# A depthwise convolution of 32 taps in front of a transformer block: as one 32x32 triangular product per channel on TensorE, in place of shifted multiply-adds

## The chip, the cores and the metric

The kernel runs on one core of a Trainium2 chip. The metric is the device time of one execution in microseconds (us). A kernel's time is the median of its runs.

## The reference

x is 32 sequences (B) of 32 tokens (T) with 256 channels (C). `cond` (32 x 256) serves twice: as the 32 taps of a causal depthwise convolution over the tokens, and as the conditioning vector of a block with attention and an MLP, one row per sequence. All is float32.

```
x  = x + conv(x, cond)               # y[b,t,c] = sum_j cond[31-j,c] * x[b,t-j,c]
ada = cond @ ada_w + ada_b           # shift, scale, gate, twice
x1 = ln(x) * (1 + scale1) + shift1
q, k, v = split(x1 @ qkv_w + qkv_b)  # 16 heads of 128
a  = softmax(q k^T / sqrt(128)) v    # within each sequence of 32
h  = x + gate1 * (a @ out_w + out_b)
x2 = ln(h) * (1 + scale2) + shift2
h  = h + gate2 * (gelu(x2 @ ffn_w1 + ffn_b1) @ ffn_w2 + ffn_b2)
x  = x + h
```

## The kernel before, in words

Activations are held with channels in the 128 partitions (two tiles, `ct`) and the 1024 tokens along the free axis. The queues of the five engines are written out by hand, each in its own block (SyncE issues the loads, then GpSimd, ScalarE, VectorE, TensorE), and tied by semaphores; each engine goes through its list in order. A large product is made of three fp32r matmuls (`three`, L927, and `v_tile`, L934) from operands split into a high and a low part: ScalarE makes the high parts (`high_parts` of the weights, L333; `x1_high`, L376), GpSimd the low parts of the weights (L278), VectorE those of the activations (`x1_low`, L595).

The 16 heads come in four groups (`hg`) of four, the tokens in two halves (`u`) of 512, so there are eight units (hg, u). A unit projects twelve banks of q, k and v, makes the scores (L992, 32x32 blocks), and in between does the attention product (`attend`, L1006) and the output projection (`out_proj`) of the unit before it. Then come the second norm, the MLP and the stores.

At the start, x is loaded with tokens in partitions, in three chunks (`CHUNKS`: 256, 256 and 512 tokens), turned by TensorE in transposes (L839, L909) and copied to `x0`. The convolution is a sum over 31 lags and the token itself. Some lags go to TensorE (`PE_LAGS`: 12, 16 and 8 by chunk) as products with a diagonal matrix (`diag`, made by ScalarE, L342, and GpSimd, L270), accumulated in a bank (L853); the others go to VectorE as multiply-adds (L537) into `xc`. `conv_sum` (L547) adds the bank. Chunk by chunk the first norm follows: `mean` on TensorE (L863), `centre` (L553) on VectorE, `squares` (L371) on ScalarE, `var` (L874, L879) on TensorE, `var_eps` (L568) on VectorE, the power -1/2 (`rstd`, L284) on GpSimd, `spread` (L891) on TensorE, `norm`, `shift` (L582, L589) on VectorE. `modulation` (L899, added up in L602) gives shift, scale and gate from `cond`. The first half of the projections of unit (0,0) is done in two pieces, `project_chunk(0)` and `project_chunk(1)`; the convolution, norm and the rest of chunk 2 lie between these and the first attention products.

The order on TensorE ahead of unit (0,1), in the program's words:

```
conv(0), transposes of chunk 2, modulation(0), mean(0), conv(1) with var(0), spread(0)
project_chunk(0) with mean(1), var(1), spread(1); conv(2, 0, 4)
project_chunk(1) with scores(0, 0); conv(2, 4, ..); modulation(1)
mean(2), attend and out_proj of (0,0) with var(2), modulation(2), spread(2)
project(0, 1, ..) nine banks; scores(0, 1); three banks
```

## Time and profile before

| | us |
|---|---|
| median of 3 runs | 338.48 |
| lowest and highest run | 337.24, 339.4 |
| profiled execution, span from first to last instruction | 337.2 |
| TensorE matmul busy | 319.7 (95%) |
| TensorE weight load busy | 269.0 (80%) |
| VectorE, ScalarE, GpSimd busy | 180.0, 152.7, 80.8 |

The profile has one line for a group of instructions: source line, engine, operation, output <- input, partitions x elements, count, then the busy time. PE is TensorE, PEld its weight load, DVE VectorE, ACT ScalarE, POOL GpSimd, SP SyncE. An ordinary fp32 matmul of the program stands in the trace as two records, a transpose or an fp32r matmul as one. PEclk is the granted TensorE clock, 1.00 at 2.4 GHz and 0.50 at 1.2 GHz. "Idle before" names what ended an engine's idle time. Matmuls overlap, so a record's own time is longer than the step from one to the next; such steps are taken from the starts.

### The profile page before, as it was taken

To read this page: it belongs to the slowest core of one execution; us is meant where nothing else is said; L and a number is where in the kernel's file an instruction comes from. 1 tells how busy PE (TensorE), PEld (TensorE's weight loads), DVE (VectorE), ACT (ScalarE), POOL (GpSimd) and SP (SyncE) were. 2 spreads that over 40 slices of the span, in tenths; PEclk is the share of its full clock that TensorE was granted. 3 is DMA by queue.
4 is the path that set the end of the run, shared out by engine and by line. 5 is a ranking of instruction groups with operands and counts; after the bars stand their busy time and mean duration, and the time that the engine had idled before them with its cause. 6 is when DMAs were issued, how large, how long until landed. Compare 5 with 4: busy or idle time off the path is not lost.

```text
span 337.2 us, 6425 instructions
## 1 busy us (share of the span) xinstructions
PE 319.7 (95%) x2655; PEld 269.0 (80%) x2655; DVE 180.0 (53%) x354; ACT 152.7 (45%) x269; POOL 80.8 (24%) x78
## 2 busy tenths in 40 slices
PE   5969599999999999999999999999999999899994
PEld 4959496868888888888888888888898778588884
DVE  4959979866606224333441532631625699783232
ACT  6421032423366525526625535653443557742910
POOL 5606510031034103006303003500201444430400
PEclk9959789999999999999999999999999999999998
DMA  7822100010004202002300101210200000000011
GB/s 247 318 68 62 62 3 0 2 65 0 0 2 126 64 0 64 0 2 68 122 0 0 62 0 41 86 63 0 64 2 0 3 2 0 0 2 0 0 64 62
DMA packets 9607, 14.56 MB, mean 43 GB/s; under 512 B 520, under 2 KB 5744, under 8 KB 9584
## 3 DMA queue, kind: packets, MB, share of 16 engines
q1 hardware_dynamic: 9536, 14.19, 12.9%
q8 instruction: 17, 0.28, 0.3%
q14 instruction: 6, 0.05, 0.1%
q10 hardware_dynamic: 48, 0.03, 0.0%
HBM read 13.18 MB, written 1.05 MB: 42 GB/s over the span
## 4 chain that ended last, share of the span: by engine, by line
PE 79%; DVE 17%; issue 1%; DMA 1%; ACT 1%; DVEq 0%
PE bank L930 16%; PE bank L931 16%; PE bank L932 16%; PE bank L1006 7%; DVE xc L537 6%; PE bank L939 4%; PE bank L941 4%; PE bank L940 4%; PE bank L863 3%; PE bank L992 3%; PE bank L853 3%; DVE pt L642 2%; DVE yacc L747 1%; DVE xc L547 1%; DMA crow<-in_cond_dram 1%
## 5 line engine op out<-in xcount | busy, mean ns | idle before, releaser
L278 POOL TENSOR_TENSOR wl<-raw,wh 128x512 fp32r<-128x512 f32 x40 | 53.1, 1349 | 181.2 <-ACT wh L333 181.2
L930 PE MATMUL bank<-x1h,wl 128*128 128x512 f32 (+1 forms) x176 | 67.8, 385 | 0.0
L931 PE MATMUL bank<-x1l,wh 128*128 128x512 f32 (+1 forms) x176 | 65.9, 374 | 0.0
L932 PE MATMUL bank<-x1h,wh 128*128 128x512 f32 (+1 forms) x176 | 65.8, 374 | 0.0
L394 ACT ACTIVATE pool<-bank,bg 128x512 f32<-128x512 f32 x56 | 38.6, 688 | 57.3 <-PE bank L932 57.0
L653 DVE SCALAR_TENSOR_TENSOR ol<-bank,bT,oh 128x512 fp32r<-128x512 f32 x32 | 23.9, 749 | 46.8 <-ACT oh L423 46.0
L537 DVE SCALAR_TENSOR_TENSOR xc<-x,condT,xc 128x240 f32<-128x240 f32 (+32 forms) x114 | 39.4, 417 | 0.0
L930 PEld LDWEIGHTS bank<-x1h,wl 128*128 128x128 f32 x176 | 34.0, 193 | 6.3 <-issue 0.7
L931 PEld LDWEIGHTS bank<-x1l,wh 128*128 128x128 f32 x176 | 34.0, 193 | 5.8 <-issue 0.2
L932 PEld LDWEIGHTS bank<-x1h,wh 128*128 128x128 f32 x176 | 33.9, 193 | 5.7
L1006 PEld LDWEIGHTS bank<-pt,pool 128*128 128x128 f32 x256 | 31.9, 191 | 3.4 <-issue 0.9
L1006 PE MATMUL bank<-pt,pool 128*128 128x128 f32 x256 | 32.8, 276 | 0.6 <-DVE ol L653 0.4
L423 ACT ACTIVATE oh<-bank,bg 128x512 fp32r<-128x512 f32 x32 | 21.9, 687 | 22.3 <-PE bank L1006 22.3
L617 DVE TENSOR_REDUCE mx<-bank 128x16 f32<-128x512 f32 x8 | 5.5, 691 | 47.2 <-PE bank L992 47.2
L853 PE MATMUL bank<-x,diag 128*128 128x256 f32 (+23 forms) x144 | 30.5, 369 | 0.0
L853 PEld LDWEIGHTS bank<-x,diag 128*128 128x128 f32 x144 | 24.8, 202 | 4.8 <-issue 1.0
L930 PE MATMUL bank<-oh,wl 128*128 128x512 f32 x64 | 26.4, 412 | 0.0
L939 PE MATMUL bank<-wh,x1l 128*128 128x512 f32 x64 | 26.3, 411 | 0.0
L941 PE MATMUL bank<-wh,x1h 128*128 128x512 f32 x64 | 25.0, 391 | 0.0
L932 PE MATMUL bank<-oh,wh 128*128 128x512 f32 x64 | 25.0, 391 | 0.0
L931 PE MATMUL bank<-ol,wh 128*128 128x512 f32 x64 | 25.0, 390 | 0.0
L940 PE MATMUL bank<-wl,x1h 128*128 128x512 f32 x64 | 25.0, 390 | 0.0
(105 smaller groups left out, 450.8 us busy)
## 6 DMA issues: line engine op xcount, KB each, us to landing
raw<-in_L_cond_qkv_w_dram SPq DMA_DIRECT2D x12, 512.0 KB, 3.8
raw<-in_L_cond_out_w_dram SPq DMA_DIRECT2D x4, 512.0 KB, 3.4
raw<-in_L_cond_ffn_w_dram SPq DMA_DIRECT2D x4, 512.0 KB, 3.4
adaw<-in_L_cond_ada_w_dram SPq DMA_DIRECT2D x1, 1024.0 KB, 11.3
out_dram<-pool SPq DMA_DIRECT2D x4, 256.0 KB, 2.2
pool<-in_x_dram SPq DMA_DIRECT2D x2, 256.0 KB, 3.1
adaw<-in_L_cond_ada_w_dram SPq DMA_DIRECT2D x1, 512.0 KB, 5.3
pool<-in_x_dram SPq DMA_DIRECT2D x1, 512.0 KB, 6.1
```

What stands on the lines that cost most here:

```text
L278: g.tensor_tensor(wl[:, cols], raw[:, cols], wh[:, cols].bitcast(F32), ALU.subtract)\
L394: a.activation(dst, src, ACT.Identity, bias=bg[:, j // GH, j % GH:j % GH + 1])\
L537: v.scalar_tensor_tensor(out=acc[:, :, j:], in0=xs[:, :, :T - j], scalar=w, in1=acc[:, :, j:], op0=ALU.mult, op1=ALU.add).then_inc(s_cdve, 1)
L653: v.scalar_tensor_tensor(out=ol[:, h, :], in0=OB[h % 2][:, :], scalar=bT[:, bass.ds(group * GH + (2 * NH + h), 1)], in1=oh[:, h, :].bitcas ...
L853: m = pe.matmul(dst[:, :, j:], diag[:, CT * d + ct, :], xs[:, :, :T - j], start=(i == 0), stop=(i == last))
L930: pe.matmul(dst, wl[:, w_cols], a_hi, start=start, stop=False)
L931: pe.matmul(dst, wh[:, w_cols], a_lo, start=False, stop=False)
L932: return pe.matmul(dst, wh[:, w_cols], a_hi, start=False, stop=stop)
L939: pe.matmul(dst, x1l[:, kt, tk], wh[:, wc], start=(kt == 0), stop=False)
L940: pe.matmul(dst, x1h[:, kt, tk], wl[:, wc], start=False, stop=False)
L941: m = pe.matmul(dst, x1h[:, kt, tk], wh[:, wc], start=False, stop=(kt == CT - 1))
L1006: m = pe.matmul(OB[h % 2][:, t * P:(t + 1) * P], v_sb[:, hn, t, h * P:(h + 1) * P], pt[:, hn, h, t, :], start=True, stop=True)
```

## The change

The convolution becomes one product per channel c: the stationary operand is the 32x32 matrix `toep[s, u, c] = cond_pad[s + u, c]` (s the input token, u = 31 - t the output token counted from the end), zero where s + u > 31; the moving operand is that channel of x in all 32 sequences, with tokens in the partitions. `cond_pad` is `cond` with 31 rows of zeros behind it, written to DRAM by two DMAs of ScalarE's queue, and `toep` is loaded from it by one DMA whose rows overlap. x is loaded once, with the 32 tokens in 32 partitions (`xs`). TensorE first puts x itself, turned, into four banks (`XB`, L821), makes the 256 products (L836) into four other banks (`CB`), four channels in four column groups, and when ScalarE and VectorE have copied these to `conv_out`, it adds them to `XB` (`turn`, L849) by products with a 0/1 matrix `pick` that restores channel and token order. ScalarE and VectorE copy two of the sums each to `xc`. The diagonals, the multiply-adds, the copies to `x0` and `conv_sum` are gone. The norms of the three chunks are then done without a convolution between them, modulations 1 and 2 are one, and unit (0,1) has the order of the later units. The loads of the biases move from SyncE's to ScalarE's queue; `toep` stands ahead of the load of `ada_w`.

```diff
-            load_x(0)
-            load_x(1)
+            sp.dma_start(xs, x.rearrange("b t c -> t b c")).then_inc(s_x, 16)
+            sp.wait_ge(s_pad, 32)
+            sp.dma_start(toep[:, :, :].rearrange("p u c -> p (u c)"),
+                         bass.AP(cond_pad, 0, [[C, T], [1, T * C]])).then_inc(s_toep, 16)
             load_adaw(0, 0, ADA1 * P)
-            load_x(2)
...
             a.dma_start(crow[:, :], cond).then_inc(s_row[0], 16)
+            a.dma_start(cond_pad[0:T, :], cond).then_inc(s_pad, 16)
+            a.wait_ge(s_zr, 1)
+            a.dma_start(cond_pad[T:2 * T - 1, :], zrows[:, :]).then_inc(s_pad, 16)
...
+            def conv_copy(k):
+
+                a.wait_ge(s_cv, k + 1)
+                a.activation(conv_out[:, CBLK * k:CBLK * (k + 1), :],
+                             CB[k][:, :].rearrange("p (s b) -> p s b", b=B), ACT.Copy).then_inc(s_co[0], 1)
+
+            def xc_copy(n):
+
+                a.wait_ge(s_sel, n + 1)
+                a.activation(xc[:, :, XCH * n:XCH * (n + 1)],
+                             XB[n][:, :].rearrange("p (k t) -> p k t", k=CT), ACT.Copy).then_inc(s_xc[0], 1)
...
-            high_parts(0, range(0, 2))
+            conv_copy(0)
+            conv_copy(2)
+            xc_copy(0)
+            xc_copy(2)
             squares(0)
-            high_parts(0, range(2, 4))
+            high_parts(0, range(0, 4))
             group_biases(0, 0, 3)
-            high_parts(0, range(4, 5))
+            squares(1)
             x1_high(0)
-            high_parts(0, range(5, 6))
+            high_parts(0, range(4, 6))
...
+            pe.wait_ge(s_x, 16)
+            for n in range(NX):
+                for i in range(CT * XB_B):
+                    ct, b = divmod(i, XB_B)
+                    pe.matmul(XB[n][:, T * i:T * (i + 1)], xs[:, XB_B * n + b, P * ct:P * (ct + 1)], ident[0:T, 0:T],
+                              start=(i == 0), stop=False, skip_group_check=True)
...
+                for s in range(CBLK):
+                    for j in range(QB):
+                        c = SLOTS * j + CBLK * k + s
+                        m = pe.matmul(CB[k][T * j:T * (j + 1), B * s:B * (s + 1)], toep[:, :, c], xs[:, :, c],
+                                      start=True, stop=True)
+                m.then_inc(s_cv, 1)
+
+            def turn(n):
+
+                if n == 0:
+                    pe.wait_ge(s_co[0], 2)
+                    pe.wait_ge(s_co[1], 2)
+                    pe.wait_ge(s_const, 4)
+                tiles = XB[n][:, :].rearrange("p (k b t) -> p k b t", k=CT, b=XB_B)
+                for b in range(XB_B):
+                    for h in range(2):
+                        m = pe.matmul(tiles[SLOTS * h:SLOTS * (h + 1), :, b, :], conv_out[:, :, XB_B * n + b],
+                                      pick[:, h, :, :], start=False, stop=(b == XB_B - 1), skip_group_check=True)
+                m.then_inc(s_sel, 1)
...
+            turn(0)
+            turn(1)
+            mean(0)
+            turn(2)
+            turn(3)
             pe.wait_ge(s_adaw[0], 16)
-            pe.wait_ge(s_btc, 1)
             modulation(0)
-            mean(0)
...
             var(0)
-            conv(1, 2, 4)
+            mean(1)
             spread(0)
-            conv(1, 4, len(PE_LAGS[1]))
+            var(1)
+            mean(2)
...
-            project_chunk(0, (0,))
-            mean(1)
-            project_chunk(0, (1, 2))
-            var(1)
-            project_chunk(0, (3,))
+            project_chunk(0, (0, 1))
             spread(1)
-            project_chunk(0, (4, 5))
-            conv(2, 0, 4)
+            project_chunk(0, (2, 3, 4, 5))
```

TensorE's queue from its first matmul, before. `pool` holds x as loaded, `crow` is `cond`, `rows` the biases.

```order
L831 MATMUL bank<-ident,crow 128x32 x2
L839 MATMUL bank<-ident,pool 128x128 x8
L853 MATMUL bank<-x,diag 128x256 x2
L853 MATMUL bank<-x,diag 128x8x26 x2
L853 MATMUL bank<-x,diag 128x8x25 x2
L853 MATMUL bank<-x,diag 128x8x24 x2
L909 MATMUL bank<-ident,pool 128x128 x8
```

And after, up to the first projection (L923).

```order
L814 MATMUL bank<-ident,crow 128x32 x2
L821 MATMUL bank<-ident,pool 128x32 x64
L825 MATMUL bank<-ident,rows 128x72
L836 MATMUL bank<-pool,toep 32x32 x256
L849 MATMUL bank<-pick,conv_out 64x2x32 x32
L866 MATMUL bank<-xc,ones 128x256 x2
L849 MATMUL bank<-pick,conv_out 64x2x32 x32
L902 MATMUL bank<-condT,adaw 128x32 x8
L877 MATMUL bank<-ones,x 128x1 x4
L866 MATMUL bank<-xc,ones 128x256 x2
L894 MATMUL bank<-ident,rs 128x128 x2
```

The eight transposes and the lag products between them are replaced by 64 + 256 + 64 small products in a row, all ahead of the modulation and of the norm of chunk 0 but for its mean.

VectorE's queue around the sum and the centring of chunk 0, before. `adaT` holds shift, scale and gate.

```order
L537 SCALAR_TENSOR_TENSOR xc<-x,condT,xc 128x8x2 x2
L537 SCALAR_TENSOR_TENSOR xc<-x,condT,xc 128x8 x2
L547 TENSOR_TENSOR xc<-xc,bank 128x256 x2
L553 TENSOR_TENSOR yacc<-xc,bank 128x256 x2
L602 TENSOR_TENSOR adaT<-bank,bT 128x128
```

And after.

```order
L532 COPY conv_out<-bank 128x512 x2
L538 COPY xc<-bank 128x2x256 x2
L555 TENSOR_TENSOR yacc<-xc,bank 128x256 x2
L604 TENSOR_TENSOR adaT<-bank,bT 128x128
L612 TENSOR_SCALAR adaT<-adaT 128x64
L563 TENSOR_TENSOR yacc<-yacc,adaT 128x256 x2
L555 TENSOR_TENSOR yacc<-xc,bank 128x256 x2
```

The centring of chunk 0 (L555) now stands behind two copies of `xc`, of which the second waits for the last turn.

## Rows read from the trace of the kernel before

**Rows 1.** The page, chain that ended last: shares by engine, then by line.
```profile
PE 79%; DVE 17%; issue 1%; DMA 1%; ACT 1%; DVEq 0%
PE bank L930 16%; PE bank L931 16%; PE bank L932 16%; PE bank L1006 7%; DVE xc L537 6%; PE bank L939 4%; PE bank L941 4%; PE bank L940 4%; PE bank L863 3%; PE bank L992 3%; PE bank L853 3%; DVE pt L642 2%; DVE yacc L747 1%; DVE xc L547 1%; DMA crow<-in_cond_dram 1%
```

**Rows 2.** Stretches: bounds, length, busy time (records) of each engine, PEclk, DMA share, GB/s.
```profile
34.27:101.29 67.02, 62.12 (x476) 51.38 (x478) 45.13 (x117) 23.45 (x45) 11.80 (x8) 0.95 0.05 17
101.29:337.20 235.91, 229.80 (x2026) 191.54 (x2026) 109.49 (x165) 116.28 (x190) 52.94 (x40) 1.00 0.10 32
```

**Rows 3.** The chain in order of time, 3 to 40 us: start, us, what.
```profile
6.90 11.95 DVE xc L537 x38
...
19.77 2.05 PE bank L863 x4
...
33.84 5.00 DVE xc L537 x22
```

**Rows 4.** Waits of TensorE, 16 to 106 us: us in total, times, longest.
```profile
PE bank L863 <- DVE xc L547: 7.6, 3, 3.8
```

**Rows 5.** TensorE in order of time, 2.4 GHz: start, us, line, shapes, records.
```profile
14.90 1.87 PE L899 MATMUL bank<-condT,adaw 128*128 128x32 f32 x16
...
51.72 5.59 PE L853 MATMUL bank<-x,diag 128*128 128x512 f32 x16
...
58.22 0.28 PE L930 MATMUL bank<-x1h,wl 128*128 128x256 f32 x1
...
62.17 0.28 PE L930 MATMUL bank<-x1h,wl 128*128 128x256 f32 x1
...
64.37 1.30 PE L992 MATMUL bank<-pool 128*32 128x32 f32 x128
...
67.10 4.37 PE L853 MATMUL bank<-x,diag 128*128 128x336 f32 x16
...
71.30 1.87 PE L899 MATMUL bank<-condT,adaw 128*128 128x32 f32 x16
...
83.72 1.06 PE L1006 MATMUL bank<-pt,pool 128*128 128x128 f32 x8
...
89.08 0.39 PE L931 MATMUL bank<-x1l,wh 128*128 128x512 f32 x1
...
94.56 0.39 PE L931 MATMUL bank<-x1l,wh 128*128 128x512 f32 x1
```

**Rows 6.** TensorE in order of time, 1.2 GHz.
```profile
42.24 0.41 PE L930 MATMUL bank<-x1h,wl 128*128 128x256 f32 x1
...
44.80 0.41 PE L930 MATMUL bank<-x1h,wl 128*128 128x256 f32 x1
```

**Rows 7.** Bytes moved in a stretch; the small load of cond, us to landing.
```profile
7.00:9.50 2.50, 2.50 (x13) 2.32 (x13) 2.50 (x6) 2.50 (x10) 2.50 (x7) 1.00 0.95 327
...
crow<-in_cond_dram ACTq DMA_DIRECT2D x1, 32.0 KB, 2.6
```

**Rows 8.** VectorE, ScalarE and GpSimd in order of time.
```profile
21.86 0.75 DVE L553 TENSOR_TENSOR yacc<-xc,bank 128x256 f32<-128x256 f32 x2 [2.23 <-PE bank L863]
...
22.96 1.13 ACT L333 ACTIVATE wh<-raw 128x512 fp32r<-128x512 f32 x2
...
13.97 2.50 POOL L278 TENSOR_TENSOR wl<-raw,wh 128x512 fp32r<-128x512 f32 x2 [2.70 <-ACT wh L333]
...
26.02 0.83 POOL L284 TENSOR_TENSOR rs<-ve,mhalf 128x2 f32<-128x2 f32 x1 [9.55 <-DVE ve L568]
```

**Rows 9.** Stretches of 1 us with their granted clock (PEclk).
```profile
17.00:18.00 1.00, 0.00 (x0) 0.00 (x0) 1.00 (x7) 0.00 (x0) 0.00 (x0) 0.94 0.37 59
...
37.00:38.00 1.00, 0.00 (x0) 0.00 (x0) 1.00 (x7) 0.00 (x0) 1.00 (x1) 1.00 0.92 346
38.00:39.00 1.00, 0.00 (x0) 0.00 (x0) 0.97 (x7) 0.00 (x0) 0.43 (x1) 0.68 0.21 78
...
73.00:74.00 1.00, 0.18 (x3) 0.10 (x2) 0.84 (x2) 0.00 (x0) 0.00 (x0) 1.00 0.73 226
```

More of the change, by code:

```diff
@@ L713, in _ @@
             softmax_transpose(0, 0)
-            conv_sum(2)
-            centre(2)
-            o_low(0, 0, (0, 1))
-            scale_up(2)
-            var_eps(2)
-            o_low(0, 0, (2,))
-            norm(2)
-            shift(2)
-            o_low(0, 0, (3,))
-            x1_low(2)
-            modulation(1)
-            modulation(2)
-            add_y(0, 0, first=True)
-            one_plus(2, SCALE2)
-            softmax_front(0, 1)
-            softmax_back(0, 1)
+            unit(0, 1, first_y=True)
             unit(1, 0, first_y=True)
@@ L862, in mean @@
+            pe.wait_ge(s_toep, 16)
+            for k in range(NX):
+                conv(k)
+            def mean(n):
+                if n >= NC:
+                    pe.wait_ge(s_in, CT * (n - NC + 1))
+                if n in (0, 2):
+                    pe.wait_ge(s_xc[0], n // 2 + 1)
+                if n in (1, 2):
+                    pe.wait_ge(s_xc[1], n)
                 for ct in range(CT):
```

274 lines of the change are left out of this document (107 added, 167 removed).

## The prediction

> **What bounds the kernel now.** I read the chain that ended last, then TensorE by stretches, then the chain in order of time at the start. The chain is 79% TensorE and 17% VectorE, and the VectorE share is mostly one line, L537, the convolution's multiply-adds [rows 1]. By stretches, everything from the scores of unit (0,1) at 101.29 to the end takes 235.91 us, with TensorE busy for 229.80 of it; from the first projection at 34.27 to those scores it is 67.02 us, busy 62.12 [rows 2]. The diff leaves the order behind 101.29 as it is, so I keep 235.91. What can change is the start (0 to 34.27) and the 67.02. The start is VectorE's: 38 multiply-adds in 11.95 us for chunk 0, then 22 in 5.00 us for chunk 1, and TensorE's mean (L863) waits for the sums behind them, 3.8 us at the longest [rows 3, 4].
>
> One execution was profiled, span 337.2 us, the same as the fastest of the three runs (337.24); their median is 338.48. I add 1.2 us to a forecast span to get a median.
>
> **Prices.** An fp32 matmul is two records of 2 cycles a column each. A record with 128 weight columns and 32 moving columns costs 1.87/16 = 0.117 us (L899). Four-wide packed ones, 32 weight columns and 32 moving columns into four column groups in turn, cost 1.30/128 = 0.010 us a record (L992). A 256-column projection record is (62.17 - 58.22)/33 = 0.12, a 512-column one (94.56 - 89.08)/24 = 0.228, and eight attention records 0.9 [rows 5]. All that is at the 2.4 GHz level. At 1.2 GHz the 256-column record, which like L899 has 128 weight columns to load, is (44.80 - 42.24)/12 = 0.213, 1.8 times as long [rows 6]; I take that for a 128-weight record at 1.2 GHz whatever its moving columns.
>
> **The change, up to the first projection (before: 34.27).**
> 1. x comes as one 1 MB DMA. The DMA engines moved 327 GB/s around here and the small load of cond lands 2.6 us after its issue [rows 7]: 0.75 + 2.6 + 1.05 MB at 327 GB/s (3.2) = 6.5 us. The padded filter is written by two DMAs of ACT's queue (issued by about 2.2, landed by about 5), then the 1 MB triangular load is issued: it shares the engines with x, 2.1 MB in all, and lands at 9 to 12 us, 15 at half that rate.
> 2. 64 transposes by matmul, now 128 records, since they are ordinary fp32 products that leave their result in the bank. Weights 128 columns, 32 moving: 0.117 each, 15.0 us, from 6.5 to 21.5. This is work that TensorE did in 16 single records before. It hides the triangular load with 6 us or more to spare; without that cover a load at 27 us would cost 5 us.
> 3. The convolution: 256 products of 32x32x32, 512 records, in the four-wide pattern of L992. That row gives 0.010 us, 5.2 us in all. But here both operands are read with a step of 1 KB between elements, which no row shows. Bounds: below 5.2 by nothing (the same columns must stream); above, no overlap of the four groups, 0.040 us, 20 us. I take 0.0146, half again the row it resembles: 7.5 us, to 29.1 (with 0.1 for the bias transpose).
> 4. Copy of the last block on VectorE, 0.65 (its centring of 256 columns is 0.38 with start-up, so 512 are put at that), then the turns: 64 products, 128 records of 64 weight and 64 moving columns in two column halves. Between 0.027 (columns alone, two at once) and 0.117; I take 0.045, 2.9 us for each half of them. Turns 0 and 1 to 32.7, mean(0) 1.0, turns 2 and 3 to 36.6.
> 5. VectorE's centre(0) is now queued behind the copy of turn 3, though its own data were ready: 36.6 + 0.65, centre two in 0.75 to 38.0. ACT's squares to 38.7; the high parts of the first weights come only behind them, 1.13 for two; POOL's low parts 1.25 each, its rstd 0.83 [rows 8]: rstd(0) at 42.8. Centre(1), the modulation and both scalings fit beside that. Spread 0.5, norm, shift, high and low parts 2.4: 45.8. TensorE has var(1) and mean(2) (1.9) in front of the projection: 46.3.
> So the first projection starts 12 us later than before. All of VectorE's multiply-adds are gone, yet at the start they are more than replaced by TensorE's 15.0 + 7.5 + 5.8.
>
> **From the first projection to the scores of (0,1) (before: 67.02).** Two project_chunks, 48 x 0.12 + 12 x 0.228 = 8.4 each, 16.8; spreads and variance between them 2.2; scores(0,0) 1.3; modulation(1) with eight chunks in one piece, 32 x 0.117 = 3.7, and 0.6 for VectorE's add that the next unit waits for; nine banks of unit (0,1) 12.5 (88.8 to 101.3 before); attention 4 x 0.9 = 3.6; output projection 24 x 0.228 = 5.5. That is 46.2. VectorE's softmax now comes behind its third norm and the modulation, and the transposed probabilities are late by an estimated 1.3: 47.5. Saved against 67.02: 19.5, made of the chunk-2 convolution (two pieces, 5.4 and 4.2 without their overlap [rows 5]), the two means of 2 us that move ahead of this stretch (4.0), TensorE's idle time (4.9) and the 1.2 GHz stretch behind it (about 1).
>
> **The sum.** 46.3 + 47.5 + 235.9 = 329.7. I add 1.1 for one stretch at 1.2 GHz: 330.8, and 1.2 for the median: 332.0 us.
>
> At step 3 the trace is silent on wide steps. The Trainium skill (Advanced Engine Details and Errata, SBUF Cachelines) says that reads are at full speed only if successive accesses hit the same 16-byte line, with a penalty otherwise. If that meant twice the price of L992, it would be 0.020 a record and 10.4 us, 2.9 more than I take. No row of this trace agrees or disagrees.
>
> **Rivals.**
> - *The small products do not raise TensorE's clock* (the other side, slower). What decides is whether TensorE runs at 1.2 GHz through the 128 transposing records and the convolution. For: TensorE is cold when x lands. It did convolution products until 14.90, then 1.87 us of 32-column records [rows 5], and about 1.1 us after those the clock fell to 1.2 GHz (0.94 in 17 to 18), whereas in a longer idle stretch after dense projection records it held 1.00 through 37 to 38 and fell only in the next us (0.68) [rows 9]. So a stretch of such records may neither hold nor raise the clock. Against: the same 1.87 us of records from 71.30 [rows 5] and 0.8 us idle cost nothing (1.00 in 73 to 74) [rows 9]; and no row shows a long stretch of them. Price: transposes 128 x 0.213 = 27.3, 12.3 more; at least the first part of the convolution at nearly double, 2.5 more: 332 + 14.8 = 347. If the convolution and turns stay low too, 355.
> - *Wide steps break the four-wide overlap*: 512 x 0.040 = 20.5, 13 more, 345. For: no row has such steps; against: L992's overlap of products that differ only in column group.
> - *A moderate price for the steps*: 0.020 a record, 335. The page named above would have it so.
> - *Weights of 32 partitions load faster than those of 128*: transposes at half price, 7.5 less, then the triangular load at 12 is the next limit: 325. The Trainium skill (TensorE: Matmul & The Clock Gate, LDWEIGHTS) speaks against it: the time goes by columns, not rows. The two 32-row transposes of this trace are too few to tell.
> - *The triangular load comes late* (it waits for a DRAM write, and reads one small piece of DRAM over and over): at 27 us 337.
>
> **How the numbers follow.** Forecast 0.38, moderate steps 0.08, fast weights 0.07, late load 0.07, clock 0.32, broken overlap 0.08. A measurement of this kernel tells about 1% from no change: below 335.1 is faster, above 341.9 slower. Faster: 0.38 less its tail, most of fast weights and some of the moderate price: 0.47. Same: late load and the near tails of both sides: 0.14. Slower: clock and broken overlap: 0.39. The forecast's own range is 326 to 337. The range goes from 324 to 350: it takes in the clock's case at its first price, and leaves out 355 and times below 324. It is wide because two cases of opposite sign hold 0.7.
>
> **What would show it.** The profile after should show 128 records of the transposing line ending near 21.5 us (near 34 by the clock's rival, with granted clock 0.5 or records of 0.21 us), convolution records over 7 to 8 us (20 if the overlap breaks), the first projection at 46, the scores of (0,1) at 94 to 95, and 236 us behind them. If TensorE waits for the triangular load, the late load is right. If what lies behind the scores differs from 235.9 by more than 1 us, my frame is wrong.

## The result, and the profile after

The changed kernel takes 368.7 us (median of 4 runs, 367.0 to 372.47), the kernel before 338.56 us in the same job: ratio 1.090, 95% interval 1.084 to 1.097. It is slower by 9%, where I had forecast 332.0 and had given 350 as the upper end of the range. One of the runs below, the 338.89 us of e9, fell in a slower state of the chip and counts in no ratio.

The page of the profiled execution (span 367.0 us), chain that ended last, shares by engine and by line:

```profile
PE 87%; DVE 7%; DMA 2%; issue 1%; ACT 1%; POOL 0%
PE bank L923 15%; PE bank L924 15%; PE bank L925 15%; PE bank L821 7%; PE bank L999 7%; PE bank L932 4%; PE bank L836 4%; PE bank L933 4%; PE bank L934 4%; PE bank L866 3%; PE bank L985 3%; PE bank L849 2%; DMA pool<-in_x_dram 2%; PE bank L902 2%; PE bank L894 1%
```

VectorE's multiply-adds [rows 1] have left the chain, as the change says they should. In their place stand L821 (transposing products, 7%), L836 (the convolution, 4%) and L849 (the turns, 2%). The two stretches that answer to [rows 2], cut at the first projection and at the scores of unit (0,1):

```profile
73.67:128.79 55.12, 51.64 (x421) 44.85 (x419) 19.76 (x35) 22.30 (x43) 11.39 (x8) 0.88 0.07 22
128.79:367.00 238.21, 230.09 (x2027) 191.67 (x2026) 109.51 (x165) 116.30 (x190) 52.91 (x40) 1.00 0.10 32
```

The last stretch is 2.3 us longer than the 235.91 of before with the same busy time, and the middle one is 11.9 us shorter than 67.02. The start went from 34.27 to 73.67: 39.4 us longer. So the loss is in the start. TensorE in order of time there (start, us, line, shapes, records, in brackets what it waited for):

```profile
7.87 27.51 PE L821 MATMUL bank<-ident,pool 32*128 32x32 f32 x128 [3.36 <-DMA pool<-in_x_dram]
...
35.63 14.31 PE L836 MATMUL bank<-pool,toep 32*32 32x32 f32 x512
50.77 4.26 PE L849 MATMUL bank<-pick,conv_out 128*64 128x64 f32 x64 [0.84 <-issue]
54.97 1.47 PE L866 MATMUL bank<-xc,ones 128*128 128x256 f32 x4
56.37 4.28 PE L849 MATMUL bank<-pick,conv_out 128*64 128x64 f32 x64
60.58 1.97 PE L902 MATMUL bank<-condT,adaw 128*128 128x32 f32 x16
...
70.89 3.76 PE L866 MATMUL bank<-xc,ones 128*128 128x512 f32 x4
```

L821 costs 27.51/128 = 0.215 us a record. That is the price of [rows 6], 0.213, at 1.2 GHz, and not the 0.117 that I took from L899 at 2.4 GHz. L836 costs 0.0279 a record (14.31/512), L849 0.067 (4.26/64). What ran beside the convolution is odd as well. The copies of its blocks out of the banks (L348, L532) and the two large loads (SyncE's queue, us to landing):

```profile
39.69 2.33 ACT L348 ACTIVATE conv_out<-bank 128x512 f32<-128x512 f32 x1 [2.96 <-PE bank L836]
43.15 2.98 DVE L532 COPY conv_out<-bank 128x512 f32<-128x512 f32 x1 [38.37 <-PE bank L836]
...
49.98 0.69 DVE L532 COPY conv_out<-bank 128x512 f32<-128x512 f32 x1 [3.86 <-PE bank L836]
```

```profile
pool<-in_x_dram SPq DMA_DIRECT2D x1, 1024.0 KB, 7.1
toep<-cond_padded SPq DMA_DIRECT2D x1, 1024.0 KB, 7.2
```

A copy of 512 columns takes 0.69 us once the convolution is over and 2.1 to 3.0 us beside it (the third, ScalarE's at 46.59, took 2.14). The triangular load was issued at 9.09 and landed at about 16.3, under the cover of L821 as forecast. In the middle stretch, windows of 2 us (the columns of [rows 2]; the number behind x counts every record that touches the window, so it is higher than the number that starts in it):

```profile
94.00:96.00 2.00, 0.01 (x2) 0.01 (x3) 0.17 (x1) 2.00 (x6) 1.24 (x2) 1.00 0.00 0
96.00:98.00 2.00, 2.00 (x129) 1.94 (x130) 0.00 (x0) 0.42 (x1) 1.27 (x2) 0.66 0.03 8
98.00:100.00 2.00, 2.00 (x6) 1.52 (x6) 0.00 (x0) 0.00 (x0) 0.00 (x0) 0.50 0.66 209
100.00:102.00 2.00, 2.00 (x20) 1.96 (x18) 0.00 (x0) 0.00 (x0) 0.00 (x0) 0.98 0.19 61
...
104.00:106.00 2.00, 1.44 (x4) 1.16 (x4) 1.82 (x4) 0.00 (x0) 0.00 (x0) 0.50 0.00 0
```

TensorE stands still for 2.9 us up to 96.0, and its waits name what for (us, times, longest):

```profile
PE bank L985 <- ACT pool L414: 2.9, 1, 2.9
```

The scores of (0,0) wait for a bank copy of ScalarE. That copy stands behind the high part of chunk 2's norm, and the high part waits for VectorE. The chain that ended last goes through that norm:

```profile
90.29 1.28 DVE yacc L584 x2
```

The clock falls behind the wait, rises, and falls once more while the modulation's 32 records run (100.2 to 104.0).

**The theories.** A: the thin products (32 rows, or 32 columns) neither raise nor hold TensorE's clock, so the whole start runs at 1.2 GHz. S: the steps of 1 KB cost what the convolution lost, and slow the copies beside it (e6 and e7 split this into S1, S2 and P). O: ScalarE's order makes the wait at 94. Rivals: the price of L821 is its own and has nothing to do with the clock ("theory B" in what was expected of e1 and e4); the convolution is bound by something other than its reads; the scores were late anyway.

### The profile page after: what moved, and what is told of

The parts are those of the page before. It is cut to its first block, busy times and chain, and to the rows that moved or that the text cites. A ratio compares the mean times of both kernels' runs of the same rounds, so it can differ in the third digit from the quotient of the medians.

```text
span 367.0 us, 7472 instructions
## 1 busy us (share of the span) xinstructions
PE 345.1 (94%) x3263; PEld 296.3 (81%) x3263; DVE 143.0 (39%) x224; ACT 152.2 (41%) x253; POOL 73.1 (20%) x64
## 4 chain that ended last, share of the span: by engine, by line
PE 87%; DVE 7%; DMA 2%; issue 1%; ACT 1%; POOL 0%
PE bank L923 15%; PE bank L924 15%; PE bank L925 15%; PE bank L821 7%; PE bank L999 7%; PE bank L932 4%; PE bank L836 4%; PE bank L933 4%; PE bank L934 4%; PE bank L866 3%; PE bank L985 3%; PE bank L849 2%; DMA pool<-in_x_dram 2%; PE bank L902 2%; PE bank L894 1%
## 5 line engine op out<-in xcount | busy, mean ns | idle before, releaser
L277 POOL TENSOR_TENSOR wl<-raw,wh 128x512 fp32r<-128x512 f32 x40 | 52.1, 1324 | 240.1 <-ACT wh L339 240.1
L923 PE MATMUL bank<-x1h,wl 128*128 128x512 f32 (+1 forms) x176 | 69.0, 392 | 0.6 <-issue 0.6
L923 PEld LDWEIGHTS bank<-x1h,wl 128*128 128x128 f32 x176 | 34.2, 195 | 7.4 <-issue 1.8
L924 PEld LDWEIGHTS bank<-x1l,wh 128*128 128x128 f32 x176 | 34.3, 195 | 6.3 <-issue 0.8
L821 PE MATMUL bank<-ident,pool 32*128 32x32 f32 x128 | 27.5, 396 | 3.4 <-DMA pool<-in_x_dram 3.4
L821 PEld LDWEIGHTS bank<-ident,pool 32*128 32x128 f32 x128 | 27.4, 328 | 3.5 <-DMA pool<-in_x_dram 3.5
L430 ACT ACTIVATE oh<-bank,bg 128x512 fp32r<-128x512 f32 x32 | 22.0, 687 | 19.5 <-PE bank L999 19.5
L923 PE MATMUL bank<-oh,wl 128*128 128x512 f32 x64 | 26.4, 412 | 0.0
L404 ACT ACTIVATE pool<-bank 128x512 f32<-128x512 f32 x28 | 16.6, 595 | 16.9 <-PE bank L934 16.9
L644 DVE STREAM_TRANSPOSE pt<-pnorm 32x512 f32<-32x512 f32 (+1 forms) x36 | 23.2, 643 | 1.2
```

Source lines behind the costliest of these rows:

```text
L277: g.tensor_tensor(wl[:, cols], raw[:, cols], wh[:, cols].bitcast(F32), ALU.subtract)\
L644: v.transpose(dst, pn[rows_b, cols].rearrange("p (n k) -> p n k", k=T)).then_inc(s_pt, 1)
L821: pe.matmul(XB[n][:, T * i:T * (i + 1)], xs[:, XB_B * n + b, P * ct:P * (ct + 1)], ident[0:T, 0:T], start=(i == 0), stop=False, skip_group ...
L923: pe.matmul(dst, wl[:, w_cols], a_hi, start=start, stop=False)
L924: pe.matmul(dst, wh[:, w_cols], a_lo, start=False, stop=False)
```

## Experiments on the start's clock

**e1_wide: 128 moving columns instead of 32 in the transposing products.** Only the right operand changes, to a slice of a shifted identity (`wide`, 896 B a partition, made by GpSimd, allocated behind `zrows`).

```diff
-pe.matmul(XB[n][:, T * i:T * (i + 1)], xs[...], ident[0:T, 0:T], ...)
+d = max(0, i - 12)
+c0 = T * (i - d)
+pe.matmul(XB[n][:, c0:c0 + P], xs[...], wide[:, T * (3 - d):T * (7 - d)], ...)
```

> The changed kernel, with the same 64 transposing products but 128 moving columns in each in place of 32 (the identity beside zeros, so that zeros are added to the neighbours); number of records, weights and results stay the same. Theory A (thin records do not raise the clock): the records are as long as before at 1.2 GHz (0.215 us), then the clock rises a few us into them, and the rest step at 0.117; the transposes take about 17 to 20 us instead of 27.5, the convolution starts near 26, and if it holds the clock it and the turns are faster too: 345 to 358 us in all. Theory B (the price is that of weights in 32 partitions, whatever the clock): 27.5 us as before, 367 to 369.

Measured: 378.68 us, ratio 1.124 (1.118 to 1.130) against before. In TensorE's order of time:

```profile
7.89 27.64 PE L829 MATMUL bank<-wide,pool 32*128 32x128 f32 x128 [3.31 <-DMA pool<-in_x_dram]
...
35.77 26.93 PE L844 MATMUL bank<-pool,toep 32*32 32x32 f32 x512
```

Four times the columns in the same 0.216 us. Theory A was expected to show a rise within these records and 17 to 20 us; there was none. The number is theory B's (27.5 us). So the moving columns do not set a record's price here, which leaves its 128 weight columns, and streaming four times the columns through 32 rows did not raise the clock. Whether there is a clock in the price at all is left to e4. The second line was not looked for: the convolution's instructions are untouched, and took twice as long. e6 takes that up.

**e4_dense_before: 24 dense 128x128x128 products ahead of x**, into a bank that is written again later.

```diff
+pe.wait_ge(s_const, 2)
+for _ in range(24):
+    pe.matmul(CB[0][:, 0:P], ones[:, :], ident[:, :], start=True, stop=True)
 pe.wait_ge(s_x, 16)
```

> 24 fp32 products of 128 columns by 128, into a bank not used then, are added on TensorE while it waits for x, from about 2 to 8 us. Theory A: the clock is at 2.4 GHz when the transposes begin, so the first of them step at 0.117 us, and within a few us they step at 0.215 again, since such records do not hold the clock; the kernel gains 1 to 3 us. Rival: once up, the clock stays up through them (all 128 at 0.117, 15 us): the kernel gains 12 us or more. Theory B: 0.215 from the first.

Measured: 367.91 us (one run). Its TensorE records, and windows (the columns of [rows 2]):

```profile
12.40 23.96 PE L825 MATMUL bank<-ident,pool 32*128 32x32 f32 x128
```

```profile
14.00:16.00 2.00, 2.00 (x21) 2.00 (x20) 0.00 (x0) 0.00 (x0) 0.00 (x0) 1.00 0.95 264
...
18.00:20.00 2.00, 2.00 (x12) 2.00 (x11) 0.00 (x0) 0.00 (x0) 0.00 (x0) 0.50 1.04 381
```

By the starts of the records, the same products, without a break, step at 0.112 us while the granted clock is 1.00 and at 0.213 while it is 0.50. That settles what 0.215 is: theory B, which had 0.215 from the first, is out. And such records do not hold a clock that they were given: it fell (0.58 in 16 to 18) although TensorE was busy all the time. The gain, 0.8 us, is under the 1 to 3 expected: the dense products ran from 4.46 and held the thin ones back until 12.40.

In the changed kernel the PEclk column reads 1.00 over the same records at 0.215. The column shows 1.00 until the first change that the trace records, so in that stretch the clock must be read from the price of a record. Read so, theory A's "whole start" is too much. The mean at 54.97 took 1.47 us, between its 1.13 at the higher clock (e3) and its 2.05 at the lower [rows 3], and L902 at 60.58 took 1.97, its price at 2.4 GHz. So the clock rose behind the first 64 records of the turns, which use all 128 rows, and fell again in 62 to 64 (0.63). In e4, where the column shows it, it rises at the same place (0.68 in 56 to 58).

**e5_full_rows: the same products with all 128 rows in use.** Rows 32 to 127 of x's tile are zeroed, both operands have 128 rows.

```diff
+g.memset(pool[T:2 * T, :], 0.0).then_inc(s_pz, 1)
+v.memset(pool[2 * T:P, :], 0.0).then_inc(s_pz, 1)
-pe.matmul(XB[n][:, T * i:T * (i + 1)], xs[...], ident[0:T, 0:T], ...)
+pool_rows = pool[:, :].rearrange("p (b c) -> p b c", c=C)
+pe.matmul(XB[n][:, c0:c0 + P], pool_rows[...], wide[:, T * (3 - d):T * (7 - d)], ...)
```

> The 64 transposing products of the changed kernel with all 128 rows of the array in use (rows 32 to 127 of x's tile are zeroed, the right operand is a 128-row slice of a shifted identity of 128 columns), everything behind them as in the changed kernel. Theory A1 (a product that fills only 32 of the 128 rows does not raise the granted clock, one that fills all of them does): the clock rises within the stretch, the later records cost 0.11 to 0.12 us and the 128 take 16 to 20 us instead of 27.5; the kernel is 8 to 10 us shorter if the convolution behind them then runs at the higher clock at first, and the convolution's records show what 2.4 GHz is worth to them. Rival A2 (it is the number of records with fresh weights, not the rows, that keeps the clock down): still 0.215 a record and 27.5 us, the clock at 1.2 GHz throughout. Placement: the extra tile moves the triangular tile by 896 B per partition, so if the convolution takes 27 us again as in the run with 128 moving columns, placement does it.

Measured: 359.81 us (one run). TensorE in order of time, then windows:

```profile
10.10 16.83 PE L835 MATMUL bank<-wide,pool 128*128 128x128 f32 x128 [5.40 <-POOL pool L277]
...
26.93 15.10 PE L850 MATMUL bank<-pool,toep 32*32 32x32 f32 x512
```

```profile
12.00:14.00 2.00, 2.00 (x11) 2.00 (x11) 0.00 (x0) 0.00 (x0) 0.00 (x0) 1.00 1.29 262
...
16.00:18.00 2.00, 2.00 (x20) 2.00 (x20) 0.00 (x0) 0.00 (x0) 0.00 (x0) 1.00 1.04 384
...
30.00:32.00 2.00, 2.00 (x80) 2.00 (x76) 0.00 (x0) 1.06 (x1) 0.00 (x0) 1.00 0.00 0
32.00:34.00 2.00, 2.00 (x78) 2.00 (x76) 0.00 (x0) 2.00 (x1) 0.00 (x0) 0.50 0.04 8
```

Theory A1 holds: with the same number of records and columns as e1, and zeros in the added rows, the records' step falls from 0.213 us (12 to 14) to 0.112 (16 to 18), and the 128 take 16.8 us instead of 27.6. What differs from e1 is the rows in use (and that `wide` lies behind `hl` here, so that the triangular tile is not moved; my remark on placement in the text above was mistaken). This is 8.9 us of the kernel, although the products start 2.2 us later, behind GpSimd's zeroing. The last two windows show two more things. The convolution's records step at 0.029 us at the granted clock 1.00 and at 0.030 at 0.50: with steps of 1 KB the clock is not its price. And the clock fell at 32 while TensorE was busy without a break since 10.1, five us into the convolution: its records of 32 rows did not hold the clock either.

**e2_no_transposes: no transposing products, and x itself left out of the sum**, to see what they cover.

```diff
-for n in range(NX):
-    for i in range(CT * XB_B):
-        pe.matmul(XB[n][...], xs[...], ident[0:T, 0:T], start=(i == 0), stop=False, ...)
-    ... pick[:, h, :, :], start=False, stop=(b == XB_B - 1), ...)
+    ... pick[:, h, :, :], start=True, stop=True, ...)
```

> The 64 transposing products are left out, so x itself is not added to the convolution. Both theories: the convolution starts when the triangular load has landed, at 16 to 17 us instead of 35.6, so the kernel takes 19 us less, about 349. If the small products themselves do not raise the clock (theory A for them too), convolution records stay at 0.028 us and turns at 0.067. If it was only the long stretch of transposes that kept it down, they fall to 0.014 and 0.04, and the time to about 337.

Measured: 351.31 us (one run), 17.4 less. TensorE now waits for the triangular load:

```profile
15.65 6.33 PE L831 MATMUL bank<-pool,toep 32*32 32x32 f32 x219 [5.62 <-DMA toep<-cond_padded]
24.00 3.76 PE L831 MATMUL bank<-pool,toep 32*32 32x32 f32 x128 [2.02 <-issue]
```

So 27.5 us of products cover 7.8 us of waiting, as the forecast's step 2 had it in kind. The convolution's records still cost 0.029 (6.33/219) and the turns' 0.065, which the text above would take for a sign of the low clock. But e5 shows the first, and e4's turns the second, at either clock, so e2 cannot tell. And in front of the second row is a wait for "issue", in which TensorE had nothing to do with any semaphore. The next runs show more of these.

## Experiments on the convolution's reads

**e3_contiguous: the same 256 products on contiguous operands** (other data, so the output is not the convolution).

```diff
-m = pe.matmul(..., toep[:, :, c], xs[:, :, c], ...)
+m = pe.matmul(..., toep_flat[:, T * c:T * (c + 1)], pool[0:T, T * c:T * (c + 1)], ...)
```

> Both operands of the convolution products are read from 32 neighbouring elements instead of with a step of 1 KB; the products are of other data, so the result is not the convolution. If the wide step costs, the 512 records fall from 14.2 us to about 10 (0.0195 each, the price of the score products at half the clock) and the kernel by about 4 us. If the clock alone makes them slow, nothing changes: 14.2 us and 368.

**e6_moved_tile: the changed kernel with an unused tile in front of the triangular one.**

```diff
 zrows = sb("zrows", [T - 1, C])
+spare = sb("spare", [T, 7 * T])
```

> The changed kernel with nothing but an unused tile of 896 B a partition in front of the triangular tile, which shifts that tile. Theory P (the price of the wide-stepped reads depends on where the two operands lie against each other): the convolution takes about 27 us instead of 14.3 (0.053 a record) and the copies beside it 3 to 5 us; the kernel is about 12 us slower than the changed one, 380 us. Rival Q (the slow convolution of the run with 128 moving columns came from what ran before it, not from the shift): 14.3 us and 368 us as in the changed kernel.

**e7_pitch_1040: steps of 1040 B in both operands.**

```diff
-xs = pool[0:T, :].rearrange("p (b c) -> p b c", c=C)
+xs = xpitch[:, :, 0:C]
+nc.sbuf_tensor("xpitch", [T, B, C + 4], F32)
-nc.sbuf_tensor("toep", [T, T, C], F32)
+nc.sbuf_tensor("toep", [T, T, C + 4], F32)
```

(The triangular load's access pattern changes with it.)

> Both operands of the convolution with a step of 1040 B between elements instead of 1024 B (rows of x and of the triangular tile padded by 4 elements, x in another place). Theory S1 (it is any step larger than a few bytes that doubles the price): 0.028 a record or more, 14 us, copies beside it still 2 to 3 us. Rival S2 (it is the power-of-two step): 0.015 a record as with contiguous operands, the stretch 8 to 12 us, the copies beside it 0.7 us, and the kernel 4 to 6 us shorter than the changed one.

Measured: e3 365.48 us, e6 381.15 us, e7 368.83 us (one run each). TensorE's records of the convolution in e3, in e6 and in e7, one fence each:

```profile
35.73 3.20 PE L838 MATMUL bank<-pool,toep 32*32 32x32 f32 x220
40.07 1.93 PE L838 MATMUL bank<-pool,toep 32*32 32x32 f32 x128 [1.14 <-issue]
43.81 1.93 PE L838 MATMUL bank<-pool,toep 32*32 32x32 f32 x128 [1.80 <-issue]
```

```profile
35.62 26.69 PE L837 MATMUL bank<-pool,toep 32*32 32x32 f32 x512
```

```profile
36.05 3.81 PE L838 MATMUL bank<-xpitch,toep 32*32 32x32 f32 x220
40.81 2.29 PE L838 MATMUL bank<-xpitch,toep 32*32 32x32 f32 x128 [0.95 <-issue]
44.54 2.26 PE L838 MATMUL bank<-xpitch,toep 32*32 32x32 f32 x128 [1.44 <-issue]
```

| step of the operands | us a record | copy of 512 columns beside it |
|---|---|---|
| contiguous (e3) | 0.0146 | 0.6 to 0.7 |
| 1040 B (e7) | 0.0173 | 0.6 to 0.7 |
| 1024 B (the changed kernel) | 0.0279 | 2.1 to 3.0 |
| 1024 B, both tiles in the same places (e2, e4, e5) | 0.029 | 2.4 to 7.2 |
| 1024 B, the triangular tile 896 B further on (e6, and e1) | 0.052 | 12.5 to 19.5 |

Theories S2 and P hold: not a wide step as such, but the step of 1024 B is dear, and how dear depends on where the tiles lie against each other. (e7 also puts x in another place; e10 goes back to 1024 B with x left there, and the records cost 0.0296.) One copy of ScalarE in e6 ran from 42.91 for 19.5 us, until the convolution was over. e1's surprise was placement: its `wide` tile had moved the triangular tile by the same 896 B.

But of the kernel's time e3 gains only 3.2 us and e7 nothing, though a record costs half or two thirds. The convolution ends only 1.9 us sooner in e3 and 0.8 in e7; the rest went into waits for "issue". (In e7 the first projection still came 1.3 us sooner, at 72.40. It lost this again behind the scores of (0,1), where TensorE waited 3.3 us for "issue" ahead of the scores' records, against 2.1 in the changed kernel.) From the start of one group of 128 records to the next is 3.74 us in e3 (43.81 - 40.07) and 3.73 us in e7: 0.029 us a record, almost exactly what the 1 KB reads cost. The first 220 records come without a break. I read this as two limits of TensorE at the same height: its reads, and the supply of its instructions. e11 and e12 test the second.

## Experiments on the order, and a kernel that beats both

**e8_copy_order: ScalarE's queue altered in one place.**

```diff
-    if j == 7:
-        x1_high(2)
-    if j == 8:
-        high_parts(0, range(6, 8))
+    if j == 9:
+        x1_high(2)
+        high_parts(0, range(6, 8))
```

> The changed kernel with ScalarE's queue altered in one place: the high part of chunk 2's norm (which waits for VectorE) and the high parts of the output weights stand behind the tenth bank copy instead of behind the eighth and ninth. Theory O (the 3.3 us for which TensorE waits ahead of scores(0,0), and the fall to 1.2 GHz behind it, come from that order of ScalarE's queue): the wait goes to under 1 us, the clock does not fall before the modulation, and the scores of (0,1) come 3 to 6 us sooner against the first projection than the 54.2 us of the changed kernel; kernel 363 to 365 us. Rival R (the copies are late anyway, because scores wait for banks, not for the norm): the wait stays over 2 us, time 368 us.

Measured: 362.04 us (one run), 6.7 less. Scores(0,0) came without a wait at 92.50, and from 78 to 98 the clock stayed up:

```profile
78.00:98.00 20.00, 20.00 (x276) 18.36 (x275) 8.94 (x18) 10.99 (x25) 4.37 (x4) 1.00 0.02 5
```

Theory O holds: from the first projection (73.41) to the scores of (0,1) (122.51) it is 49.1 us now, 6.0 less than 55.1. Of these 2.9 are the wait; the rest I put down to the clock, which stood at the lower level for some 10 us between 96 and 111 and for 3.4 here. The kernel, at 362.04, is a little below the 363 to 365 expected. A short fall (0.81, then 0.50 from 100 to 102) is left behind the modulation.

**e9_folded: all of this put to use.** x is folded into the filter (the last tap plus 1.0), so that no transposing product is left; steps of 1040 B; turns with contiguous weights; e8's order; the modulation under the triangular load; the high parts beside the convolution; centre(0) ahead of the copy of the fourth turn, mean(2) behind spread(1). The modulation is in three parts (bound to banks YB[0], YB[1], YB[0]). The cut shows some of the places only.

```diff
+v.tensor_scalar(crow1[:, :], crow[:, :], ident[0:T, T - 1:T], None, ALU.add)
+sp.dma_start(cond_pad[0:T, :], crow1[:, :])
-nc.sbuf_tensor("conv_out", [P, SLOTS, B], F32)
+nc.sbuf_tensor("conv_out", [P, B, SLOTS], F32)
...
+modulation(0)
...
-modulation(0)
 var(0)
 mean(1)
 spread(0)
 var(1)
-mean(2)
+modulation(1)
```

> A kernel that keeps the change's convolution but takes out what the runs found dear: x itself is folded into the filter (1.0 added to its last row), so the 64 transposing products go; both operands have a step of 1040 B; the turns read contiguous weights; the padded filter is written from 32 and 16 partitions, the modulation of the first norm runs while the triangular load is under way, the weights' high parts run beside the convolution, centre(0) stands ahead of the fourth copy, mean(2) behind the second projection, ScalarE's bank copies ahead of chunk 2's high part. Expected: triangular load landed at 14, convolution 12 us (to 26), turns 8.4 us or less (4 to 6 if their price was the 128 B step of the weights), first projection at 44 to 48, scores of (0,1) 46 to 50 us behind it, 236 to 238 behind those: span 328 to 335, median 329 to 336, against 338 for the kernel before and 368.7 for the changed one. If the convolution is held by the supply of instructions rather than by its reads, its 512 records end no sooner than 8.5 us after the first 220 whatever the step. Rival: TensorE is now at 1.2 GHz from the start until the first projections, since nothing ahead of them raises the clock, and a second fall behind them costs another 3 to 5 us: 338 to 342, no gain on the kernel before.

Measured: 333.03 us (330.48 to 338.89, 4 runs), ratio to the kernel before 0.984 (0.975 to 0.993): faster than before by 1.6%, with anything from 0.7 to 2.5% left open, and 10% faster than the change as made. Span of the profiled execution, the fastest of the four, 328.7. TensorE in order of time:

```profile
17.30 3.53 PE L835 MATMUL bank<-xpitch,toep 32*32 32x32 f32 x203 [3.18 <-DMA toep<-cond_padded]
24.59 2.29 PE L835 MATMUL bank<-xpitch,toep 32*32 32x32 f32 x128 [3.76 <-issue]
...
34.34 3.68 PE L848 MATMUL bank<-pick,conv_out 128*64 128x64 f32 x64 [1.18 <-issue]
...
39.01 2.09 PE L848 MATMUL bank<-pick,conv_out 128*64 128x64 f32 x64
...
47.05 0.37 PE L926 MATMUL bank<-x1h,wl 128*128 128x256 f32 x1
```

First projection at 47.05, the scores of (0,1) at 93.14, 235.6 us behind them. The turns tell a further thing: in the changed kernel 64 records took 4.1 to 4.3 us in every run (e4's at either level), here 3.68 and then 2.09. Between the two the mean (L862) took 1.13 us, its price at the higher clock (2.05 where the column shows 0.50), so the clock had risen by the end of the first 64. Once their weights are contiguous (before: a step of 128 B) the turns cost 0.033 us and follow the clock. That they start a sum here and do not add to one is not it: in e2 they start one too, and took 4.17 and 4.19. Not as expected: the triangular load landed at 17.3 and not at 14. It was issued at 9.83, when the write of the padded filter, issued at 5.05 behind the load of x, had landed. And the first wait for "issue" is 3.76 us here, when in e3 and e7 it was about 1.

**e10_folded_1024: e9 with the 1024 B step put back.**

```diff
-nc.sbuf_tensor("xpitch", [T, B, C + 4], F32)
-nc.sbuf_tensor("toep", [T, T, C + 4], F32)
+nc.sbuf_tensor("xpitch", [T, B, C], F32)
+nc.sbuf_tensor("toep", [T, T, C], F32)
```

> The folded kernel (e9) with one thing put back: the step of both operands of the convolution is 1024 B again. Theory S2 (the power-of-two step is what costs): records of 0.028 to 0.053 us where they were 0.0174, the copies beside them 2 us or more instead of 1.15, and the convolution ends 3 to 10 us later than in e9 (33.2 there). Rival W (in this kernel the convolution is held by the supply of instructions, so slower records only fill the gaps): the convolution ends within 1.5 us of e9's and the kernel's span within 2 us of 328.7.

Measured: 334.69 us (one run).

```profile
16.03 6.01 PE L835 MATMUL bank<-xpitch,toep 32*32 32x32 f32 x203 [2.88 <-DMA toep<-cond_padded]
23.84 8.95 PE L835 MATMUL bank<-xpitch,toep 32*32 32x32 f32 x309 [1.79 <-issue]
```

The records cost 0.029 again, but the convolution ends at 32.8 against 33.2, and the first projection comes at 46.88. The first half of rival W holds: here the step is worth nothing at the convolution, since the slower records fill the time in which the instructions come. The load landed 1.3 us sooner, which gave the convolution that much of a start.

The copies beside these records, expected at 2 us or more, were not slowed at all:

```profile
20.02 1.02 ACT L352 ACTIVATE conv_out<-bank 128x512 f32<-128x512 f32 x1 [10.46 <-PE bank L835]
```

The last one, when the convolution was over, took 1.04. So the step of 1024 B by itself does not slow other engines' copies. Between the changed kernel and e10 the places of both tiles and the order in which the copies write differ; which of them matters was not tested.

The second half of W, a span within 2 us of e9's, failed: it was 332.8. Of the 4.1 us, 1.9 came between the first projection and the scores of (0,1), where the clock fell to 0.54 and 0.61 from 72 to 76 (1.00 in e9), and 2.3 behind those scores, of which 2.1 are one wait for "issue" ahead of a later unit's scores. The waits ahead of the clock's fall show no difference between the two, so what tipped it stays open. And e9's own runs, as far as they count, reach from 330.48 to 334.88, so one run at 334.69 does not show e10 to be slower.

**e11_held_loads and e12_loads_last: e9 with the loads of the first weights held** until two blocks of the convolution are done (e11, shown), or all four (e12, a wait for 4; with the high parts and low parts moved behind).

```diff
+sp.wait_ge(s_cv, 2)
 load_group(0)
```

> The folded kernel (e9) with the loads of the first weights and of the rest of the modulation's weights issued only when the second block of the convolution is done, so that nothing but the triangular load moves while the convolution's first products run. Theory F (TensorE's instructions are fetched by the same DMA engines, and the weights' 380 GB/s held them up): the gap of 3.8 us behind the first 203 records shrinks to 1 to 2 us, the convolution ends 2 us or more sooner than at 33.2, and the span is about 2 us below 328.7 if the weights still land in time for ScalarE. Rival G (the supply has its own rate, whatever else moves): the gap stays at 3 to 4 us, the end of the convolution the same, and the span the same or longer.

> The folded kernel (e9) with the same loads held until all four blocks of the convolution are done, and the work that needs them moved behind: the first two pairs of high parts behind ScalarE's first copy of xc, the third behind its second, and GpSimd's rstd(0) ahead of the third pair of low parts. Theory F (the supply of TensorE's instructions and the loads share the DMA engines; e9 had a gap of 3.8 us while the loads moved at 380 GB/s, e11 had 1.0 and 1.4 us until they were let go and 5.6 us then): no gap inside the convolution is over 1.8 us, it ends at 28.5 to 30 instead of 33.2, the turns behind it may be held up by up to 2 us, first projection at 43 to 45 instead of 47.05, span 325 to 327, median 326 to 330. Rival H (the loads only move the gap once more: the turns and means wait for their instructions for 3 us or more): the first projection again at 46 to 48 and the span 328 to 332.

Measured: e11 334.46 us (331.8 to 335.62; ratio to before 0.986, 0.980 to 0.992), e12 334.86 us (333.5 to 337.17; 0.989, 0.986 to 0.992). The convolution in e11, then in e12:

```profile
21.63 2.30 PE L836 MATMUL bank<-xpitch,toep 32*32 32x32 f32 x128 [0.99 <-issue]
...
33.20 1.10 PE L836 MATMUL bank<-xpitch,toep 32*32 32x32 f32 x53 [5.57 <-issue]
```

```profile
28.90 1.10 PE L838 MATMUL bank<-xpitch,toep 32*32 32x32 f32 x53 [1.44 <-issue]
```

Neither is faster than e9 (333.03). But theory F's mechanism holds. With the loads held, the first wait shrinks from 3.76 to 0.99 us. Let go at 22.8 in e11, they bring one of 5.57 us, so that the convolution there ends at 34.3 and not, as expected, 2 us before e9's 33.2. Held to the end (e12), none is over 1.5 us and the convolution ends at 30.0. So loads that move at up to 390 GB/s hold up what TensorE waits for when it waits for "issue". That this is its instructions, coming through the same DMA engines, fits a queue of the page; which engine's instructions the queue carries the page does not say. In the changed kernel (packets, MB, share of the engines):

```profile
q8 instruction: 22, 0.36, 0.4%
```

The 3 us of e12 did not reach the end, and I put that down to my order. ScalarE and TensorE in e12:

```profile
38.10 1.15 ACT L345 ACTIVATE wh<-raw 128x512 fp32r<-128x512 f32 x2 [2.62 <-DMA raw<-in_L_cond_qkv_w_dram]
...
39.91 1.26 PE L876 MATMUL bank<-ones,x 128*128 128x1 f32 x8 [2.41 <-ACT x L381]
```

I had put the second pair of high parts ahead of the squares. It waits 2.6 us for its late weights, the squares stand behind it, TensorE waits 2.4 us for them, and the clock falls: 0.66 in 40 to 42 and 0.50 from 42 to 54. The first projection came at 49.5, where 43 to 45 were expected. No run has these loads held with the squares ahead of the high parts.

## Why the prediction was wrong

Forecast span 330.8, measured 367.0: 36.2 more. By the steps of the prediction:

| step | forecast | measured | off by |
|---|---|---|---|
| 1, x lands | 6.5 | 7.9 | 1.4 |
| 2, transposing products | 15.0 | 27.5 | 12.5 |
| 3, convolution with the bias transpose | 7.6 | 14.6 | 7.0 |
| 4, last copy, turns, mean(0) | 7.5 | 10.7 | 3.2 |
| 5, from there to the first projection | 9.7 | 13.0 | 3.3 |
| first projection to scores of (0,1) | 47.5 | 55.1 | 7.6 |
| behind those, and the 1.1 added | 237.0 | 238.2 | 1.2 |

**Step 1**: x took 7.1 us from its issue, where the 327 GB/s of [rows 7] had given 5.8.

**Step 2 failed, and it was the choice of a level.** The record's price was about right at both levels (0.117 and 0.213 forecast; 0.112 and 0.213 in e4); I took 2.4 GHz. The evidence against was in my own rows: TensorE was cold when x landed, and L899's records at 14.90 were followed by a fall [rows 5, 9]. I weighed that as a rival at 0.32, with its mechanism and its price of 12.3 us, which is what step 2 lost to within 0.2. e4 and e5 show the mechanism. The rival also had the convolution slower by the clock, and the convolution was slower, but for another reason: at this step its records cost the same at both levels (e5). What the rival's 347 and 355 lacked is in the other rows of the table.

**Step 3 was mis-sized**: 0.0279 a record, between the 0.0146 that I took and the 0.040 of the upper bound, nearer neither. I wrote that no row shows such a step; the run that shows it is e3 against the changed kernel. The moderate rival had 0.020. That e3's contiguous records cost just the 0.0146 that I took is chance: mine was the L992 row and half of it again, at 2.4 GHz, and e3's ran at the lower clock. What I had not thought of: the price depends on placement and nearly doubles again in e6 and e1 (above my upper bound); the copies of other engines are slower beside such records in every run but e10; and the instructions have a rate of their own, a term that I had put at nothing. With it the convolution takes 12.3 us (35.73 to 48.02) even in e3, at my own price a record.

At that step the Trainium skill (Advanced Engine Details and Errata, SBUF Cachelines) speaks of full speed only for successive accesses in one 16-byte line. The runs agree only in part: steps of 1040 B miss such a line just as steps of 1024 B do, and cost 0.0173 against 0.0146, while 1024 B costs 0.0279 to 0.052. The rule does not tell these apart; the measurement decides.

**Step 4**: the turns cost 0.067 a record where I took 0.045. e9 shows why: their weights had a step of 128 B, and without it the first 64 cost 0.0575 and the next 0.033.

**Step 5** is in part the clock once more, which had fallen in 62 to 64: behind the power -1/2 on GpSimd, mean(2) took 3.76 us for 1.9, and the spread 1.23 for 0.5, which makes 1.9 of the 3.3 us. The other 1.4 lie ahead of it. GpSimd waited 1.43 us for the variance; VectorE takes it up behind centre(1), and that stood behind mean(1), 2.05 us long at the low clock. I had let centre(1) fit beside the rest there.

**The middle stretch**: 6.0 of its 7.6 us are the wait for ScalarE's copies and the clock behind it (e8). I had costed ScalarE's new order at nothing there, and had named no work that hides it. The forecast had one stretch at 1.2 GHz in it, and there were three.

**Right**: the triangular load is hidden by the products in front of it (landed at 16.3 against 9 to 15), VectorE's multiply-adds leave the path, and the four-wide overlap stays (0.028 against 0.040). VectorE's third norm does not leave the path: the wait at 94 goes back to it.

**The frame** of 235.9 us behind the scores missed by the forecast's own sign, which was 1 us: it took 238.2. The busy time is the same, and 2.1 of the 2.3 us are one wait for "issue" ahead of the scores of a later unit:

```profile
183.63 2.09 issue
```

e9 has no such wait, and 235.6; e10 and e11 have 2.1 us of it, e7 3.3.

e9 has its first projection at 47.05, its scores 46.1 us behind and 235.6 us behind those, where the forecast had 46.3, 47.5 and 235.9. The first of these agreements is luck. e9 has none of the transposing products, for which the forecast had 15.0 us; its convolution starts at 17.30 instead of 21.5 and takes 15.9 us instead of 7.5. So e9 shows that the design can be made to win a little, and not that the forecast's sum for the start was sound.

## What to carry to other kernels

Before replacing vector work with many small TensorE products, price them at the clock that the products themselves leave behind: records that use 32 of 128 rows ran at 1.2 GHz for all of 27 us here and lost the higher clock when they were handed it. A long run of small products is also bound by the rate at which it is issued (0.029 us a record, and 4 to 6 us of waiting where large loads move at the same time), so cutting a product's own time below that gives little: e3 halved it, and the convolution ended 1.9 us sooner. Fold an identity into the filter before making a product for it. And when an operand is read with a step, try another step and another place for the tile: 1040 B for 1024 B took a record from 0.0279 to 0.0173 us here.

## What was not expected of the hardware

- Steps of 1024 B cost 0.0279 or 0.052 us a record by where the two tiles lie, steps of 1040 B 0.0173, contiguous reads 0.0146; beside the dear ones a copy of 512 columns out of a bank took 2.1 to 19.5 us on ScalarE and VectorE instead of 0.69, but in e10, at 1024 B too, it was not slowed.
- At 1024 B the convolution ran at the same rate at either granted clock: 0.029 and 0.030 us a record (e5).
- Zeros in the other 96 rows raised the clock: 16.8 us for 27.6 (e5 against e1).
- After some 200 to 220 records a run of small products stops for 1 to 2 us every 128 records; with 390 GB/s of loads beside it for 3.8 us, and 5.6 us at the longest. The scores' packed records behind (0,1) meet such waits too, one or two of 1.6 to 2.4 us, in the changed kernel, e2, e3, e5 to e8 and e10 to e12, and not in e1, e4, e9 or the kernel before.
- A load of 1 MB into 32 partitions took 7.1 to 7.2 us from issue to landing, 146 GB/s with its start-up counted. In the windows that it filled, the core moved 258 to 262 GB/s; in those of the weights behind it 385 to 402.
